# One core, fused conv-attention blocks: the last image pair runs one stage ahead of its old place, with two buffers for x1, x2 and LN2's shifted planes

## What is computed

```python
# block L0
xn = layernorm(x, over the 32 columns)                     # LN1
q, k, v = conv3x3(conv1x1(xn))                             # three times
x1 = conv1x1(attention over channels, 8 heads) + x
xn = layernorm(x1, over the 32 columns)                    # LN2
gate = gelu(conv3x3(conv1x1(xn)))                          # 64 channels
info = conv3x3(conv1x1(xn))                                # 64 channels
x2 = conv1x1(gate * info) + x1
# block L1, on x2
out = lrelu(instance_norm(conv3x3(x2) + b))
out1 = conv3x3(out); mask = sigmoid(conv3x3(out)); xm = out * mask
q, k, v = 1x1 convs of xm (k, v zero padded)
attn = softmax over the 3x3 neighbours of q * k
out2 = sum over the neighbours of attn * v
result = x2 + out1 * mask + (1 - mask) * out2
```

## Time and profile before

| | |
|---|---|
| median of 3 runs | 241.42 us (241.01 to 241.47) |
| the profiled execution's own time | 240.31 us |
| its span in the trace | 238.5 us |
| busy: PE, DVE, ACT, POOL | 197.5, 182.1, 126.1, 69.9 us |
| from the end of the two steps (162.2 us) to the last DVE instruction (236.1 us) | 73.9 us |

### The profile page before, as it was taken

How to read it: one execution, slowest core, us unless ns; L and a number is a source line. 1 busy time by engine, 2 the same in 40 slices (tenths; PEclk the granted TensorE clock), 3 DMA queues, 4 the chain that set the end, 5 groups by cost and what they waited for, 6 DMA issues and landing times.

```text
span 238.5 us, 4801 instructions
## 1 busy us (share of the span) xinstructions
PE 197.5 (83%) x1868; PEld 112.5 (47%) x1868; DVE 182.1 (76%) x399; ACT 126.1 (53%) x252; POOL 69.9 (29%) x60
## 2 busy tenths in 40 slices
PE   0598968889487999997888989978979997967992
PEld 0338467344257456544473556442444534545741
DVE  7698977795698999997989958459994348893462
ACT  2152342552574847477755575177546568545641
POOL 8434002204008025600093232001917200404232
PEclk9999999999999999999999999999999999999999
DMA  6411021000420000010002000000010000000101
GB/s 197 93 33 47 12 77 47 0 0 0 100 77 3 0 13 0 3 33 3 0 0 91 4 9 1 0 3 0 0 47 12 3 0 0 4 0 12 48 0 47
DMA packets 9576, 6.06 MB, mean 25 GB/s; under 512 B 7568, under 2 KB 7792, under 8 KB 9552
## 3 DMA queue, kind: packets, MB, share of 16 engines
q1 hardware_dynamic: 9312, 5.16, 7.7%
q10 hardware_dynamic: 240, 0.58, 0.8%
HBM read 3.30 MB, written 1.05 MB: 18 GB/s over the span
## 4 chain that ended last, share of the span: by engine, by line
DVE 52%; PE 25%; issue 9%; ACT 8%; POOL 4%; DMA 1%; ACTq 0%; SPq 0%; DVEq 0%; POOLq 0%
PE ps L1251 9%; DVE sh_in L292 7%; POOL ln_s L411 4%; DVE sh_ln L307 3%; ACT sh_x L512 3%; DVE sh_ln L292 3%; DVE ln_out L794 3%; PE ps L1288 2%; DVE ln_s L775 2%; DVE ln_d L784 2%; DVE gi L896 2%; PE ps L1259 2%; DVE ln_d L769 2%; DVE ln_c L766 2%; DVE ln_s L764 2%
## 5 line engine op out<-in xcount | busy, mean ns | idle before, releaser
L411 POOL TENSOR_TENSOR ln_s<-ln_s,neg_half 128x16 f32<-128x16 f32 x8 | 23.3, 2911 | 93.1 <-DVE ln_s L777 93.1
L1251 PE MATMUL ps<-sh_ln,w_gi 96*128 96x512 f32 x96 | 42.4, 596 | 1.5 <-ACT v L533 1.5
L512 ACT ACTIVATE sh_ln<-ln_out 32x512 f32<-32x512 f32 (+1 forms) x40 | 24.9, 621 | 25.9 <-DVE ln_out L802 14.7
L1171 PE MATMUL ps<-busy 128*128 128x512 bf16 x130 | 34.0, 402 | 0.3 <-DVE sm L849 0.3
L1251 PEld LDWEIGHTS ps<-sh_ln,w_gi 96*128 96x128 f32 x96 | 17.9, 190 | 23.5 <-issue 23.3
L1288 PE MATMUL ps<-sh_in,w_in 128*32 128x256 f32 x384 | 22.1, 380 | 3.2 <-DVE sh_in L292 3.2
L1198 PE MATMUL ps<-w_qk,sh_ln 128*128 128x128 f32 x192 | 23.7, 278 | 1.3 <-DMA sh_ln<-ln_out 0.7
L1198 PEld LDWEIGHTS ps<-w_qk,sh_ln 128*128 128x128 f32 x192 | 22.4, 192 | 2.5 <-issue 1.7
L896 DVE TENSOR_TENSOR gi<-ps,gate 64x512 f32<-64x512 f32 x16 | 11.1, 694 | 14.3 <-ACT gate L547 14.1
L1171 PEld LDWEIGHTS ps<-busy 128*128 128x128 bf16 x130 | 13.1, 106 | 18.1 <-issue 8.4
L547 ACT ACTIVATE gate<-ps 64x512 f32<-64x512 f32 x16 | 9.1, 583 | 18.0 <-PE ps L1251 18.0
(11 more groups left out here) (135 smaller groups left out, 341.4 us busy)
## 6 DMA issues: line engine op xcount, KB each, us to landing
sh_ln<-ln_out SPq DMA_DIRECT2D x18, 64.0 KB, 2.1
x_norm<-in_x SPq DMA_DIRECT2D x4, 256.0 KB, 2.9
x_res<-in_x SPq DMA_DIRECT2D x4, 256.0 KB, 2.5
out_x<-out_s SPq DMA_DIRECT2D x4, 256.0 KB, 2.0
kc<-in_shape_consts ACTq DMA_DIRECT2D x1, 450.0 KB, 6.7
w3b<-in_w_gi SPq DMA_DIRECT2D x1, 288.0 KB, 6.4
xm<-xm SPq DMA_DIRECT2D x8, 25.5 KB, 1.9
vec<-in_vectors SPq DMA_DIRECT2D x1, 131.5 KB, 3.6
```

The source lines that it names most:

```text
L411: nc.gpsimd.tensor_tensor(ln_s[n][:, 3, :], ln_s[n][:, 2, :], neg_half[:, :], ALU.pow)\
L512: return nc.scalar.activation(o, i, ACT.Copy)
L1171: nc.tensor.matmul(ps[:, bank, at:BANK], busy[:, 0:P], busy[:, 0:BANK - at], start=True, stop=True)
L1251: mm = nc.tensor.matmul(ps[:, GI_BANKS[2 * i + h], :], w_gi[:, dy, :, :].rearrange("p m o -> p (m o)"), xs[:, i, y:y + H // 2, 0:W], start ...
```

## The change

Three tiles get a second buffer: x1, x2 and the planes `sh_ln2` are picked by `pair % 2`. With that, in `step(1, False)`, LN2 of pair 3 is done, which the tail did before: `attn_out(3)` on PE stands ahead of `window_scores(1)`, in place of three filler matmuls; `ln2_center(3)` on DVE ahead of `window_softmax(1)`; `ln_var`, `ln_apply` and the 12 shifted copies stand between the other operations on DVE and ACT. On POOL `final(1)` goes ahead of `inorm_rstd(2)`.

In the tail the gate convolution of pair 3 is spread between pair 2's `conv1`, the averages and `mask_conv`, in place of 29 filler matmuls, and `reduce_1(3)` stands in the middle of `mask_conv(2)`. Pair 3's `conv1` follows directly on pair 2's `conv2`. Pair 3's local attention gets banks 0 to 3, conv2 of it bank 6; `v_evac` moves from DVE to ACT for both pairs. Two waits are relaxed: `masked` waits for the readers of xm rather than for `window_v`, and `x2_sum` no longer waits for the residual of the pair before.

```diff
-        x1 = sb("x1", [P, 2, BLK])
-        x2 = sb("x2", [P, 2, BLK])
+        x1, x2 = [[sb(f"{t}_{n}", [P, 2, BLK]) for n in (1, 2)] for t in ("x1", "x2")]
-        sh_ln2 = sb("sh_ln2", [3 * C, 2, PLANE])
+        sh_ln2 = [sb(f"sh_ln2_{n}", [3 * C, 2, PLANE]) for n in (1, 2)]
...
         def conv2_bank(early):
-            return 1 if early else 7
+            return 6 if early else 7
+        def q_bank(early):
+            return 0 if early else 4
+        def sims_bank(early):
+            return 2 if early else 5
+        def values_banks(early):
+            return (1, 0) if early else (7, 4)
...
 # POOL, step(pair, norm) where norm is false
-                rstd(1, pair + 2)
-                inorm_rstd(pair + 1)
-                scaled_weights(pair + 1)
-                final(pair)
+                    rstd(1, pair + 2)
+                    final(pair)
+                    inorm_rstd(pair + 1)
+                    scaled_weights(pair + 1)
...
 # ACT, the tail
-            load_exp_table()
-            squares(1, last)
-            conv1_evac(but_last)
-            in_planes(but_last)
-            ln2_planes(last)
+            gelu(last, 0)
+            conv1_evac(but_last)
+            gelu(last, 1)
+            in_planes(but_last)
+            gelu(last, 2)
+            gelu(last, 3)
+            load_exp_table()
+            x2_planes(last)
             tanh_mask(but_last)
             out1_evac(but_last)
-            gelu(last, 0)
-            gelu(last, 1)
+            conv1_evac(last, True)
             q_evac(but_last)
             k_evac(but_last)
-            gelu(last, 2)
-            gelu(last, 3)
+            in_planes(last)
             key_windows(but_last)
-            x2_planes(last)
             window_exp(but_last)
-            conv1_evac(last, True)
-            in_planes(last)
             tanh_mask(last, True)
+            v_evac(but_last)
+            q_evac(last, True)
+            k_evac(last, True)
+            key_windows(last)
             probs_t(but_last)
+            out1_evac(last, True)
+            window_exp(last)
+            v_evac(last, True)
             pv_evac(but_last)
-            q_evac(last)
-            k_evac(last)
-            key_windows(last)
-            window_exp(last)
-            out1_evac(last, True)
-            probs_t(last)
+            probs_t(last, True)
...
 # DVE, step(pair, norm) where norm is false, and masked
+                    ln2_center(pair + 2)
                 window_softmax(pair)
...
+                    ln_apply(1, ln2_out, "ln2", pair + 2)
+                    gated(pair + 1, 0)
+                    gated(pair + 1, 1)
+                    ln2_copies(pair + 2, [(1, r) for r in range(R - 1)])
+                    gated(pair + 1, 2)
+                    ln2_copies(pair + 2, [(0, 0)])
+                    gated(pair + 1, 3)
+                    ln2_copies(pair + 2, [(0, 1), (0, 2), (0, 3)], done=True)
...
-                dve.wait_ge(g_v.sem, g_v.before(pair))
+                if not is_first(pair):
+                    dve.wait_ge(g_xw.sem, g_xw.done(pair - 1))
+                    dve.wait_ge(g_k.sem, g_k.done(pair - 1))
```

More of the change, by code:

```diff
@@ L308, in slot_copies, with ln2_planes_free @@
             return ins
+        def ln2_planes_free(engine, pair):
+            if pair > 1:
+                engine.wait_ge(g_i.sem, g_i.done(pair - 2))
         def slots_free(engine, pair):
@@ L567, in out1_evac, with q_evac @@
                   .then_inc(g_o1.sem, 1)
-            def q_evac(pair):
+            def q_evac(pair, early=False):
                 act.wait_ge(g_q.sem, g_q.done(pair))
@@ L581, in k_evac, with v_evac @@
                     nc.scalar.activation(k_h[:, i, :, :].rearrange("p y x -> p (y x)"),
-                                         ps[:, 5 + i, 0:(RH + 2) * PW], ACT.Identity,
+                                         ps[:, sims_bank(early) + i, 0:(RH + 2) * PW], ACT.Identity,
                                          bias=vec[:, V_BK:V_BK + 1]).then_inc(g_k_sb.sem, 1)
+            def v_evac(pair, early=False):
+                act.wait_ge(g_v.sem, g_v.done(pair))
+                act.wait_ge(g_pv.sem, g_pv.before(pair))
+                for h in range(2):
+                    nc.scalar.activation(v_t[:, 4 * h:4 * h + 4, :].rearrange("p u m -> p (u m)"),
+                                         ps[:, values_banks(early)[h], :], ACT.Copy).then_inc(g_v_sb.sem, 1)
             def key_windows(pair):
@@ L601, in window_exp, with probs_t @@
                     nc.scalar.activation(pr, pr, ACT.Exp).then_inc(g_we.sem, 1)
-            def probs_t(pair):
+            def probs_t(pair, early=False):
                 act.wait_ge(g_pv.sem, g_pv.before(pair))
@@ L622, in ln2_planes @@
             def ln2_planes(pair):
-                planes("ln2", ln2_out, sh_ln2, g_ln[1], g_i, pair)
+                ln2_copies(pair, [(1, R - 1)] + [(2, r) for r in range(R)], done=True)
             def x2_planes(pair):
-                planes("x2", x2, sh_x2, g_x2, g_c1, pair)
+                planes("x2", x2[pair % 2], sh_x2, g_x2, g_c1, pair)
             def in_planes(pair):
@@ L1111, in _ @@
             but_last, last = PAIRS - 2, PAIRS - 1
-            ln2_center(last)
-            ln_var(1, last)
+            gated(last, 0)
             inorm(but_last)
@@ L1135, in _ @@
             in_planes(last)
-            v_evac(but_last)
-            window_probs(but_last)
+            window_softmax(but_last)
             scaled_act(last)
             masked(last)
-            q_evac(last)
-            window_softmax(last)
+            window_probs(but_last)
+            q_evac(last, True)
+            window_softmax(last, True)
             window_probs(last)
-            v_evac(last)
             final(last)
@@ L1351, in window_scores, with probs_transposed @@
                     mm.then_inc(g_s.sem, 1)
-            def probs_transposed(pair):
+            def probs_transposed(pair, early=False):
                 for t in range(UNITS // 2):
@@ L1362, in probs_transposed, with window_out @@
                         mm.then_inc(g_t.sem, 1)
-            def window_out(pair, busy_for=0):
-                stay_busy(busy_for, 5)
+            def window_out(pair, early=False):
                 pe.wait_ge(g_t_sb.sem, g_t_sb.done(pair))
```

221 lines of the change are left out of this document (132 added, 89 removed).

## The result

The changed kernel takes 228.73 us (median of 4, 227.94 to 229.47) against 241.21 us of the kernel before (median of 4): a ratio of 0.9461, 95% interval 0.9408 to 0.9514. Twice more, beside the experiments on two other chips, it took 228.14 us (ratio 0.9419, 0.9385 to 0.9454) and 228.17 us (0.9406, 0.9354 to 0.9458), where the kernel before took about 242.4. The forecast was 229.0 us in a range of 225.0 to 233.0. So the gain was 12.5 us on the first chip and 14.2 on the two others, against 12.4 forecast; the three intervals of the ratio overlap.

What follows compares the result with a forecast made beforehand. No engine was taken as the bound, but the latency of one pair's stages. Terms of -16.5, +0.6 and +3.5 us made 12.4 less, so 241.42 became 229.0 us, range 225.0 to 233.0.

Steps and rivals of the forecast that it cites:

- What bounds the kernel: Whole program: no engine is the bound; the latency of one pair's stages sets the end, with x2(3) at 195.34 us.
- LN2 in step 1: Step 1: stalls beside POOL cost DVE 1.5 us; softmax(1) starts at 144.8, conv1(2) at 164.75, 2.3 us late.
- the walk: All engines: instructions followed in the new order, each starting when engine, inputs and buffers are there, with the old durations.
- The gate in the tail: Tail: gate matmuls hide in_planes(2) of 3.39 us; mask_conv(2) begins at 176.25, x2(3) at 178.85, 16.5 us earlier.
- Pair 2 pays, local attention of pair 3: Tail: xm(2) slips from 181.2 to 184.65; xm(3) ends at 199.8, softmax(3) starts at 207.95, 15.9 us earlier.
- The end: Program end: POOL's residual(3), bunched behind final(2), ends at 222.1; DVE's final(3) starts 4.3 us after window_out(3).
- The sum: Whole span: -16.5, +0.6 and +3.5 us give 226.1 instead of 238.5, 12.4 us less.
- rival 4: Tail: with less filler the granted clock falls to 1.2 GHz; all chain matmuls slow gives 250 us; chance 0.04.
- Rival 3: Tail: late halos, 1.5 us for each of two, and more POOL-DVE strife; 231.5 us, with all 234; chance 0.20.
- Rivals 2 and 5: First: POOL's branch doesn't decide the end, 224.7 us, chance 0.08; second: unseen wait of 3 to 10 us, 235, chance 0.08.

Runs made afterwards that it cites:

- ln2_early_only: Changed kernel with two buffers, early LN2 of pair 3 and POOL's new order kept, but the tail's old order without LN2: 240.53 us, ratio 0.9937 to the kernel before.
- pool_order_back: Changed kernel with final(1) on POOL again behind inorm_rstd(2) and the scaled weights: 229.82 us, ratio 0.9484 to the kernel before.
- old_banks: Changed kernel with pair 3's local attention in the old banks and old order: 229.13 us, ratio 0.9455 to the kernel before.
- residual_first: Changed kernel with omm and res in two buffers, a scratch tile for residual, and residual(3) ahead of final(2) on POOL: 224.88 us, ratio 0.9291.
- pv_first: Changed kernel with pv_evac(2) ahead of v_evac(3) on ACT, nothing else: 227.46 us, ratio 0.9383 to the kernel before.
- fill_setup: Changed kernel with 14 more filler matmuls in TensorE's idle time ahead of pair 0's reduce_1 in the setup: 227.69 us, ratio 0.9383.
- no_tail_filler: Changed kernel without the last 16 filler matmuls of the tail: 229.20 us, ratio 0.9430 to the kernel before.
- change_again: The changed kernel itself, run once more beside the experiments on another chip: 228.14 us, ratio 0.9419 to the kernel before.

## Why the prediction held

*What bounds the kernel*: right. The end is set by the latency of pair 3's stages, and x2(3) is their marker.

*LN2 in step 1*: right in place, a little too large in size. x1(3) started at 142.16 - 1.84 = 140.3 (and at 140.33 in ln2_early_only, which lost no clock ahead of it); the stalls beside POOL cost 1.42 where I took 1.5. One operation lost 0.46 and the next 0.96, while POOL's worked beside them; the one row I had gave only the second. By the Trainium skill ("SBUF — State Buffer", Who interferes with whom) a DVE operation with two inputs in SBUF and a POOL operation that reads SBUF contend for one interface, and the one that was first holds the other up; the trace agrees: POOL's two operations there took 1.73 and 1.60 instead of 1.27, in turn with DVE's. conv1(2) started at 163.9 instead of 164.75, so step 1 was 0.9 us less late than forecast (1.4 instead of 2.3). This is the term that was mis-sized. softmax(1) was 0.3 us earlier than walked. From there to the end of window_probs(1) DVE took 7.6 us, as before, where the walk had 0.3 more for `ln_var`: its two operations went wholly into the old gap. LN2's output was then 0.75 earlier than walked and probs_t(1) on ACT 1.0; it releases window_out(1), behind which conv1(2) stands.

*The gate in the tail*: right. in_planes(2) took 3.39 as taken, and the gate hid it; mask_conv(2) began at 175.4 (walk 176.25), x2(3) at 178.05 (walk 178.85), 17.3 us earlier instead of 16.5. pool_order_back shows that the 3.39 is due to POOL's order and is worth 1.65 us. ln2_early_only gets 1.9 of the 14 us, and old_banks, with the gate in its new place and pair 3's local attention in the old, gets nearly all of them: so the gain is the gate's place, with conv1(3) behind it.

*Pair 2 pays, local attention of pair 3*: right to within 1.5 us: xm(3) ready at 198.55 (walk 199.8), softmax(3) at 206.5 (walk 207.95). Of the 1.4 us, 0.8 stood already at x2(3); the other 0.6 lie in this stretch and were not traced to single instructions.

*The end*: right. POOL's branch ended 4.2 us after TensorE's (forecast 4.3). residual_first shows it by taking that branch off the path, pv_first by moving its start. What the forecast didn't see is that this branch takes back all that the new banks gain at full clock (old_banks).

*The sum*: the span fell by 12.3 us, forecast 12.4, and that it fits to 0.1 is luck: two errors of 1.8 us cancel. By terms, without the clock: x2(3) came 17.3 us earlier (forecast 16.5); from there to softmax(3) it took as long as before, 28.5 (forecast 0.6 more); and behind softmax(3) 3.1 us were lost (forecast 3.5). That is 14.2 less. The clock, a term that the sum had at nothing, took back 1.84. Its reason was that the trace of before has the full clock everywhere; but other executions of before don't (spans of 238.2 to 242.0 with a mean clock of 1.000 to 0.977), and most of the changed kernel's don't. On the two chips where such executions of before are in its median, the gain is the 14.2 of the terms.

*The rivals*: rival 4, the clock, was at work in a small form, not in the tail that I had named but behind an idle time of the setup, which was there before. I had written that no idle time of the walk is long enough for it; TensorE's 3.1 us of the setup lie outside the walk. In the tail it can happen too: fill_setup, old_banks and no_tail_filler have drops there. Rival 3's late halos didn't come (both landed after 1.9 us); its strife between POOL and DVE did beside pair 3's norm (one small operation 0.54 longer). Rivals 2 and 5 fell.

## What to carry to other kernels

When no engine is the bound, find the marker at which the last unit of work enters its serial part, and ask only how much earlier a change lets it enter. Double buffers and early LN2 alone bring little (1.9 of 14 us here); they pay by what they allow into the waiting time. A shortened branch pays only while it is the last one: the new banks took 4 us off TensorE's branch and put POOL's behind it. After such a gain look at once at what was bunched up at the end: here four elementwise operations that need nothing of pair 2's result had slid behind it, and turning two calls round with second buffers gave another 3.3 us.

## What was not expected of the hardware

The granted clock fell to about half for some 6 us after TensorE had stood idle for 3.13 us in the setup. Behind the same idle time it stayed full in another execution of the same kernel, and in the profiled one of the kernel before. It also fell behind shorter waits: 1.92 us (change_again), 1.95 (old_banks), 1.32 (no_tail_filler), and in fill_setup where TensorE had waited 1.30 and 0.93 us with one microsecond of work between. By the estimate made above, at most one of the 16 executions of the changed kernel was free of it while TensorE had work. So one profile doesn't tell whether a kernel keeps its clock.

The same instruction stream, cut at two of its own instructions, repeats to 0.05 us (80.09, 80.14, 80.12) while the executions scatter by 1 us and more. For questions under one per cent that distance was the better measure, as long as the clock is full inside it, and the clock has to be looked up for each: 80.82 looked like a loss, and by my estimate was a drop of the clock.
